# Weighted sums of two slots in one block of strips, in two attention stages of a fused decoder

## The reference

```
# causal: 16 heads of 8 features, 128 queries x 128 keys of one sequence
scores = einsum('bhqd,bhkd->bhqk', q, k) / sqrt(8) + alibi_and_causal_mask
out    = einsum('bhqk,bhkd->bhqd', softmax(scores), v) @ Wo + bo
# rotary: 16 heads of 8 features, 128 queries x 77 context keys
q, k   = rope(rms_norm(q)), rope(rms_norm(k))
out    = einsum('bhts,bhsd->bhtd', softmax(q k^T / sqrt(8)), v) @ Wo
x      = layernorm(x + out)        # after each of them
```

## Time and profile before

| | |
|---|---|
| median of three runs | 2772.31 us (2766.38 to 4171.66) |
| the profiled execution | 2773.75 us, its span 2772.0 us |
| busy over the span | PE 2534.0 (91%), DVE 1904.9 (69%), POOL 1694.9 (61%), ACT 1671.0 (60%) |
| strips L1040, causal | 2048 matmul records, 285 ns mean, 109.0 us busy |
| strips L1040, rotary | 2048 matmul records, 286 ns mean, 109.7 us busy |
| causal, from the first strips to the last | 1314.2 to 1819.4 us of the span |
| rotary, from the first strips to the last | 1867.2 to 2396.0 us of the span |

### The profile page before, as it was taken

How to read it: one execution, slowest core, us unless ns; L and a number is a source line. 1 busy time by engine, 2 the same in 40 slices (tenths; PEclk the granted TensorE clock), 3 DMA queues, 4 the chain that set the end, 5 groups by cost and what they waited for, 6 DMA issues and landing times. The chain is left out here.

```text
span 2772.0 us, 61590 instructions
## 1 busy us (share of the span) xinstructions
PE 2534.0 (91%) x19168; PEld 1864.5 (67%) x19168; DVE 1904.9 (69%) x5298; ACT 1671.0 (60%) x4543; POOL 1694.9 (61%) x2110
## 2 busy tenths in 40 slices
PE   8998999999999289996999999969999999699996
PEld 6665887877877289993555555547766666458993
DVE  6884677787777355555777777765788886445655
ACT  6773666666665234444766666639888887623334
POOL 3442334555555645554888888846688887724675
PEclk9998999999999699998999999979999999899998
DMA  8932467777774122214100000000011010011336
GB/s 260 338 107 68 151 215 226 234 224 224 223 220 129 54 65 71 72 58 129 58 11 9 9 11 9 7 25 13 16 30 30 30 30 17 30 30 54 93 93 194
DMA packets 274799, 267.86 MB, mean 97 GB/s; under 512 B 30060, under 2 KB 253561, under 8 KB 274096
## 3 DMA queue, kind: packets, MB, share of 16 engines
q1 hardware_dynamic: 256912, 228.42, 27.2%
q0 software_dynamic: 17280, 34.13, 3.6%
q10 hardware_dynamic: 288, 1.38, 0.2%
HBM read 101.24 MB, written 151.85 MB: 91 GB/s over the span
## 5 line engine op out<-in xcount | busy, mean ns | idle before, releaser
L779 POOL TENSOR_TENSOR wide_probs<-wide_exps,wide_inv_sum 128x616 f32<-128x616 f32 x128 | 168.3, 1315 | 305.6 <-DVE wide_inv_sum L1580 293.0
L749 POOL TENSOR_TENSOR causal_exps<-causal_biased,causal_neg_max 128x512 f32<-128x512 f32 x256 | 262.8, 1036 | 76.4 <-DVE causal_neg_max L1594 76.2
L758 POOL DMA_INDIRECT sorted_x<-send,place_i x240 | 244.1, 1017 | 84.2 <-ACT send L1233 44.0
L1289 ACT ACTIVATE rotary_exps<-banks,rotary_neg_max 128x77 f32<-128x77 f32 x1024 | 248.7, 341 | 19.3 <-DVE rotary_neg_max L1594 19.1
L1764 POOL DMA_INDIRECT results<-gelu_tile_out,gelu_dest_i x142 | 140.1, 986 | 142.2 <-DVE gelu_tile_out L1920 120.0
L1539 DVE TENSOR_TENSOR causal_biased<-banks,regions 128x512 f32<-128x512 f32 x256 | 163.6, 680 | 80.7 <-PE banks L1115 80.4
L1764 POOL DMA_INDIRECT results<-swiglu_tile_out,swiglu_dest_i x142 | 144.6, 1019 | 116.7 <-DVE swiglu_tile_out L1915 59.4
L1833 ACT ACTIVATE gelu_hidden<-banks,gelu_slot 128x256 f32<-128x256 f32 x284 | 116.6, 470 | 159.5 <-PE banks L2010 159.4
L1258 ACT ACTIVATE causal_exps<-causal_exps 128x512 f32<-128x512 f32 x256 | 161.2, 630 | 71.4 <-POOL causal_exps L749 71.4
L1594 DVE TENSOR_REDUCE rotary_neg_max<-banks 128x4 f32<-128x308 f32 x256 | 121.7, 475 | 113.5 <-PE banks L1129 105.1
L1273 ACT ACTIVATE causal_probsT<-banks 128x512 f32<-128x512 f32 x256 | 151.6, 592 | 79.3 <-PE banks L1140 79.3
(11 more groups left out here) (385 smaller groups left out, 7018.3 us busy)
## 6 DMA issues: line engine op xcount, KB each, us to landing
v_dram<-wide_staged SPq DMA_DIRECT2D x38, 1024.0 KB, 4.4
sorted_x<-blank SPq DMA_DIRECT2D x1, 34848.0 KB, 116.8
sorted_x<-blank SPq DMA_DIRECT2D x24, 1452.0 KB, 8.7
wide_folded<-v_dram SPq DMA_DIRECT2D x128, 256.0 KB
gelu_tile_in<-sorted_x SPq DMA_DIRECT2D x71, 132.0 KB, 2.1
swiglu_tile_in<-sorted_x SPq DMA_DIRECT2D x71, 132.0 KB, 2.1
gelu_back<-results SPq DMA_DIRECT2D x16, 512.0 KB, 8.0
swiglu_back<-results SPq DMA_DIRECT2D x16, 512.0 KB, 5.4
```

Of the source, the lines that this page charges most:

```text
L749: pool.tensor_tensor(exps[:, (NU * pair.c + m) % ES], biased[:, m % BS].rearrange("p (h n) -> p h n", h=HU), neg_max[:, m % SLOTS].unsquee ...
L758: pool.indirect_dma_start(route["sorted_x"], bass.IndirectOffsetOnAxis(ap=r_place_i[:, b % 2, which, n // 2:n // 2 + 1], axis=0), send[:, ...
L779: pool.tensor_tensor(probs[:, half % SLOTS, 0:HH * NK].rearrange("p (k h) -> p h k", h=HH), exps[:, half % EB], inv_sum[:, half % SLOTS].u ...
L1289: last = act.activation(exps[:, (NU * c.c + k) % ES, h], scores[:, h * NK:(h + 1) * NK], ACT.Exp, bias=neg_max[:, k % SLOTS, h:h + 1])
```

## The change

PE sums two slots in one block: late_sums does slots n - 1 and n, eight matmuls, at every second slot, and counts two at its end. probsT gets four slots. In causal the block moves: it stands directly behind the scores of the even slots, ahead of the transposes, with PLAG 5 instead of 4; the third of the projections goes from slot 3 to slot 4; and the transposes back with their divide go from slots 4 and 6 to 5 and 6. In rotary the block stays where it was, at even slots only, and the slots of the divide stay.

```
-        probsT = sb("probsT", [P, 2, HU * P if late else CHUNKS * P])
+        probsT = sb("probsT", [P, 4, HU * P] if late else [P, 2, CHUNKS * P])
...
-                    "causal": [(0, 0), (1, 0), (2, 0), (3, 1)], "rotary": [(5, 0), (7, 0)]}[kind]
+                    "causal": [(0, 0), (1, 0), (2, 0), (4, 1)], "rotary": [(5, 0), (7, 0)]}[kind]
...
-        TLAG, PLAG, OLAG = {"wide": (4, 5, 6), "causal": (3, 4, 5), "rotary": (2, 3, 4)}[kind]
+        TLAG, PLAG, OLAG = {"wide": (4, 5, 6), "causal": (3, 5, 5), "rotary": (2, 3, 4)}[kind]
+        DIVIDE_AT = (5, 6) if kind == "causal" else (4, 6)
...
-            def late_sum(pair, n):
-                b, j = divmod(n, UB)
-                g, odd = divmod(j, 2)
+            def late_sums(pair, n):
+                b, g = n // UB, n % UB // 2
                 pe.wait_ge(probsT_done, pair.count(NU, n + 1))
-                if n == 0:
+                if n == 1:
                     pe.wait_ge(front_done, pair.count(FU, FU))
-                if j == 0 and pair.back(1).real:
+                if n % UB == 1 and pair.back(1).real:
                     pe.wait_ge(o_done, pair.back(1).count(2, b + 1))
-                for h in range(HU):
-                    strip = 272 * 2 * b + 256 * odd + 32 * (4 * g + h)
-                    last = pe.matmul(o_bank[b][32 * h:32 * h + 32, g * P:(g + 1) * P], values[0:NK, pair.c % 2, strip:strip + 32],
-                                     probsT[0:NK, n % 2, h * P:(h + 1) * P], start=odd == 0, stop=odd == 1)
-                last.then_inc(pv_done, 1)
+                for odd in range(2):
+                    for h in range(HU):
+                        strip = 272 * 2 * b + 256 * odd + 32 * (4 * g + h)
+                        last = pe.matmul(o_bank[b][32 * h:32 * h + 32, g * P:(g + 1) * P], values[0:NK, pair.c % 2, strip:strip + 32],
+                                         probsT[0:NK, (n - 1 + odd) % 4, h * P:(h + 1) * P], start=odd == 0, stop=odd == 1)
+                last.then_inc(pv_done, 2)
...
+                    at = lagged(c, u, k, PLAG)
+                    if kind == "causal" and at is not None and k % 2 == 0:
+                        late_sums(*at)
                     at = lagged(c, u, k, TLAG)
...
-                    if late and u is not None and k in (4, 6):
-                        turn_back(u, (k - 4) // 2)
+                    if late and u is not None and k in DIVIDE_AT:
+                        turn_back(u, DIVIDE_AT.index(k))
...
-                    if at is not None and late:
-                        late_sum(*at)
+                    if at is not None and kind == "rotary" and k % 2 == 0:
+                        late_sums(*at)
...
-                        if before(pair, n, 2) is not None:
-                            bc, bk = before(pair, n, 2)
+                        if before(pair, n, 4) is not None:
+                            bc, bk = before(pair, n, 4)
                             act.wait_ge(pv_done, bc.count(NU, bk + 1))
-                        act.activation(probsT[0:NK, n % 2], p_bank[n % 2][0:NK], ACT.Copy).then_inc(probsT_done, 1)
+                        act.activation(probsT[0:NK, n % 4], p_bank[n % 2][0:NK], ACT.Copy).then_inc(probsT_done, 1)
...
-                    if u is not None and late and k in (4, 6):
-                        divide(u, (k - 4) // 2)
+                    if u is not None and late and k in DIVIDE_AT:
+                        divide(u, DIVIDE_AT.index(k))
```

## The result

The changed kernel takes 2803.02 us (median of 4 runs, 2801.22 to 2807.96) against 2773.64 for the kernel before: ratio 1.0122, 95% interval [1.0102, 1.0143]. The ratio is that of the fast runs, without one of the kernel before that took 4171.66 us. The forecast was 2784, within 2742 to 2830: a little slower, as it came out. Two of its terms were off, though, both to the same side, so the step itself came out larger than forecast.

A forecast was written before the change was run, and what follows sets the result against it. Causal was taken as bound by a 16.06 us loop over POOL, DVE and PE, rotary as paced by PE; 2773.75 + 30 (causal) - 19 (rotary) = 2785 profiled, so 2784 as median, range 2742 to 2830.

The forecast's parts named there:

- The loop: Causal pair: a chain of steps over POOL, DVE and PE sums to 16.06 us, the whole period, and sets the pace.
- rival (e): PE is the pace of causal and everything freed is gained in causal and rotary: 84 us, 2688; chance 0.07.
- The blocks on the loop: Causal, scores of slot 0 to slot 2: merging blocks gains nothing, 4.36 becomes 4.38 us, since L844 starts 0.58 later.
- The divide: Causal, first divide moved to slot 5: costs 0.49 itself, and X is held by POOL's keys; 1.00 us a pair together.
- the 0.38: Causal on DVE: length in us taken for an X row not held by POOL, against 0.53 for a held one.
- neg_max and its two buffers: Causal: DVE's neg_max of slot 5 waits for POOL's L749 of slot 3 because of two buffers; step of 1.13 us.
- Rival (d): Causal: PE idleness of some 2.4 us ahead of output transposes lowers the clock; all 29 pairs +48, 2832; chance 0.13.
- the two signs of being wrong: Causal pairs under 16.07 us with POOL free of its 1.46 us wait, or a granted clock of 0.5 in causal.
- the forecast 30: Causal as a whole: (0.02 + 1.00) x 29 periods, +30 us; +15 with the lower end.
- (a): Main case: the loop as read and half the gain in rotary, 2785 profiled, 2784 as median; chance 0.50.
- the middle, 0.6: Rotary: gain per pair taken between ends 0 and 1.2 us; over 31 periods, -19 us.
- rival (c): Rotary is ACT's at once and gains nothing: +30, 2802; chance 0.10.

The follow-up runs named there:

- Experiments 2 and 3: First: changed kernel with x's transposes and ACT's copy of them first in causal, 2833.46 us; second: that plus slot 7's probability transposes made four times, 2779.32 us.
- experiment 5: Changed kernel with four buffers of neg_max in causal instead of two, X rows left at slots 5 and 6: 2805.88 us, ratio 1.0125.
- experiment 1: Changed kernel with causal's first divide back at slot 4 and third projection back at slot 3: 2766.29 us, ratio 0.9990 against the kernel before.
- experiment 2: Changed kernel with the transposes of x, and ACT's copy of them, ahead of those of the probabilities in causal: 2833.46 us, ratio 1.0241.

## Why the prediction was right, and where not

**The loop.** Right. It was read as 16.06 before, its forecast sum is 17.08, and it measures 17.10 by the same steps. That PE was busy 95% of the time did not matter; rival (e) is out: PE is busy less and the pair is longer. Of the 1.6 us a pair that the sum frees on PE its busy time shows 0.94; nothing in the forecast for causal hung on that term.

**The blocks on the loop.** Right: 4.38 forecast between scores 0 and 2, 4.39 measured, the block of sixteen 0.64 long, and the wait of half a microsecond ahead of L844 is there (0.40 on PE's matmuls, ended by ACT's xT). Experiments 2 and 3 take it away and the pair loses 0.63.

**The divide.** Right, both halves: 0.49 for itself and half a microsecond for X, which L703 holds as L749 does. The Trainium skill's rule on the shared port pair ("SBUF — State Buffer", Who interferes with whom) is what the rows show: of the 64 X rows of causal in the changed kernel all 60 that start while an L749 or L703 runs end 0.08 to 0.09 us after it. One reading of the earlier trace rows was off: the 0.38 is not X alone. That X, too, starts within an L749 (the second of the two from 1553.90, to 1555.92) and ends 0.09 after it; the four rows of the kernel before that start with POOL free take 0.34 to 0.35. The step of 1.00 doesn't change by it, since it goes by the ends.

**neg_max and its two buffers.** The number, 1.13, was right, its cause only half. X of slot 5 ended at the same moment in the earlier trace rows, and I took the buffers alone. Nothing in the sum hung on it, but whoever had added buffers on my word would have got nothing (experiment 5).

**The clock.** Rival (d) came in part, and with it one of the two signs of being wrong that the prediction names, a granted clock of 0.50 in causal. PE's idleness ahead of the output transposes is 2.04 where 2.4 was forecast, and five of the first 28 pairs paid 1.3 to 2.4 each: 8 us of the 10 that causal has over the forecast 30. Most of the rest lies in the last three periods (38.5 for 35.0), one of which has a sixth such stretch. The forecast of (a) has none of it.

**Rotary.** Here the prediction failed: "I take the middle, 0.6: 31 periods between 32 pairs, -19 us". Ahead of the routing pairs did go from 15.69 to 15.18 (15.1 forecast). With the routing four pairs went from 67.98 to 67.71, 0.07 each, and most pairs are of that kind. PE's busy time fell by 0.78 a pair ahead of the routing and by 0.60 with it, where the sum frees 1.2; whether the rest is short waits within it was not taken apart. So rotary gave 4.6 in place of 19 in the profiled execution. Single groups of four take up to 3.3 us more than these (71.32 before, 71.03 after), in either kernel; with each of the 31 periods at its shortest over the traces of either rotary (two of the old one, seven of the new) the gain is 5.8, of it 4.3 in the first seven. And in experiment 1, whose causal is all but that of before, the whole kernel gained 3, which the runs can hardly tell from nothing. It is rival (c) for the routed pairs: most of PE's freed time became waiting, and the wait that grew is that for ACT ahead of the router (0.3 to 2.6 over four pairs). The number that spoke for it, ACT busy for 59.11 of 67.98, stood in the text beside the 0.6, and I used one figure for both kinds of pair.

The forecast for the profiled execution was 2785, +11, and its own time is 2802.4: +14 more from rotary, +10 from causal, most of it the clock, -6 from what stands ahead, which no line of the change touches, and -1 between the stages. By the number rival (c), 2802 with a chance of 0.10, comes closer than (a). That is in part luck: it has neither the clock nor the -6, and the pairs ahead of the routing did gain.

## What to carry to other kernels

Follow the loop through the pair, not the busiest engine: here a step that only moved by one slot cost 1.00 us a pair, while the work taken off the engine that is busy 95% of the time gave nothing until two ties of DVE to POOL were cut at once. Where a gain is forecast on one engine, write it down stage by stage against the next busiest engine of that stage. And look at the granted clock where TensorE is left idle just ahead of its critical run: with 2.04 us of it experiment 2 lost more by the clock than its edit saved, with 1.04 experiment 1 lost nothing.

## What the hardware showed unexpectedly

- The same idleness of 2.04 us ahead of L1063 brought the lower clock in 5 of 28 pairs of one kernel and 26 of 28 of another; with 1.04 or 0.73 there it came in none. Each such stretch of these two kernels lasted 3.4 or 6.8 us, and the pair took 1.3 to 3.2 us longer. Idle PE time filled with repeated transposes made a kernel 54 us faster.
- A DVE X row of the changed kernel that starts while POOL's L703 or L749 (1.03 us) runs ends 0.08 to 0.09 after it, whichever of the two it is: 0.89 within L703, 1.06 within L749, 0.34 alone.
